# Decoder blocks on one core: attention stacks filled by copies inside SBUF, and Mamba's sum, decays and inputs later in the issue order

## What is computed

```python
# attention with 16 heads of 8 dims: L1x, L2x, L3x (keys and values of the context), L3a (rotated), softmax
scores = jnp.einsum('bhsd,bhtd->bhst', qh, kh) / scale
attn = jax.nn.softmax(scores, axis=-1)
out = jnp.einsum('bhst,bhtd->bhsd', attn, vh)
# L0a: causal linear attention, also with 16 heads of 8 dims (phi(x) = elu(x) + 1)
# L2a: Mamba, forward and backward in time, 256 channels, 16 states
def step(h, inp):
    d, b, c, ut = inp
    dA = jnp.exp(d[:, :, None] * A)
    h = dA * h + (d * ut)[:, :, None] * b[:, None, :]
    y = jnp.einsum('bdn,bn->bd', h, c)
    return (h, y)
```

## Time and profile before

| what | value |
|---|---|
| median of three runs | 4762.9 us (4759.52 to 4770.97) |
| the profiled execution, its own time | 4766.72 us |
| its span | 4764.2 us |
| PE busy | 3496.6 us (73%) |
| DVE busy | 2955.6 us (62%) |
| ACT busy | 1970.0 us (41%) |
| POOL busy | 1234.1 us (26%) |
| mean granted TensorE clock | 0.833 of full speed |
| moved by DMA | 328.00 MB, mean 69 GB/s |

### The profile page before, as it was taken

One profiled execution on the slowest core, in us unless ns is written; L12 is line 12 of the kernel. 1 busy time (PEld: TensorE's weight loads), 2 busy tenths in 40 slices (PEclk: granted clock), 3 DMA queues, 4 the chain that ended last, 5 costly groups with the idle time before them and its releaser, 6 DMA issues. The chain is left out here.

```text
span 4764.2 us, 69288 instructions
## 1 busy us (share of the span) xinstructions
PE 3496.6 (73%) x25546; PEld 2337.3 (49%) x25546; DVE 2955.6 (62%) x6919; ACT 1970.0 (41%) x3470; POOL 1234.1 (26%) x1568
## 2 busy tenths in 40 slices
PE   5868867666878878665886887856589698685674
PEld 3645635334665555433575654533357465352353
DVE  4436874884554785577545488477654548738646
ACT  2423545343343444543344355434235335443333
POOL 0001451550000243253000045145100005516410
PEclk7989978777988988777898998877789799786776
DMA  7110121313121021032122112122211200211321
GB/s 237 46 47 14 39 81 42 103 55 106 66 79 62 28 76 58 29 130 73 47 100 69 39 36 81 45 88 84 104 56 52 98 10 28 80 54 45 117 101 49
DMA packets 174905, 328.00 MB, mean 69 GB/s; under 512 B 13260, under 2 KB 114988, under 8 KB 173740
## 3 DMA queue, kind: packets, MB, share of 16 engines
q1 hardware_dynamic: 174572, 323.59, 20.1%
HBM read 231.87 MB, written 91.67 MB: 68 GB/s over the span
## 5 line engine op out<-in xcount | busy, mean ns | idle before, releaser
L1881 PE MATMUL bank<-sb_big,sb_weights_const 128*128 128x512 f32 x512 | 376.6, 826 | 333.9 <-DVE sb_big L2119 333.2
L1434 POOL TENSOR_TENSOR sb_rs<-sb_ve,sb_weights_const 128x4 f32<-128x4 f32 x112 | 113.4, 1012 | 1757.6 <-DVE sb_ve L1420 1757.3
L1997 POOL TENSOR_TENSOR sb_big<-sb_big 128x512 f32<-128x512 f32 x384 | 496.4, 1307 | 244.9 <-DVE sb_big L2097 244.3
L1958 ACT ACTIVATE bank<-sb_big,sb_Aneg 128x512 f32<-128x512 f32 x512 | 351.7, 689 | 497.4 <-DVE sb_big L2114 392.3
L1252 DVE TENSOR_REDUCE sb_small<-bank 128x4 f32<-128x308 f32 (+1 forms) x512 | 265.9, 523 | 344.5 <-PE bank L967 340.9
L2114 DVE TENSOR_TENSOR_SCAN sb_big<-bank,sb_big 128x512 f32<-128x512 f32 x384 | 464.6, 1210 | 6.6 <-ACT bank L1958 6.3
L988 PE MATMUL bank<-sb_big 128*77 128x128 bf16 (+1 forms) x2560 | 358.1, 234 | 83.7 <-DMA sb_big<-key_parts 30.3
L988 PEld LDWEIGHTS bank<-sb_big 128*77 128x77 bf16 (+1 forms) x2560 | 274.2, 117 | 140.2 <-issue 89.8
L967 PE MATMUL bank<-sb_big 128*128 128x77 bf16 (+1 forms) x2048 | 187.4, 227 | 179.5 <-DMA sb_big<-query_parts 114.2
L1677 PEld LDWEIGHTS bank<-sb_weights_L1f,sb_big 128*128 128x128 f32 x2048 | 257.3, 191 | 109.0 <-issue 104.9
L1137 ACT ACTIVATE sb_big<-bank 77x512 f32<-77x512 f32 (+1 forms) x352 | 207.9, 593 | 228.3 <-PE bank L1009 152.4
(11 more groups left out here) (344 smaller groups left out, 8111.7 us busy)
## 6 DMA issues: line engine op xcount, KB each, us to landing
sb_big<-query_parts SPq DMA_DIRECT2D x160, 512.0 KB, 6.5
sb_big<-state_rows SPq DMA_DIRECT2D x128, 512.0 KB, 3.8
query_parts<-sb_big SPq DMA_DIRECT2D x120, 384.0 KB, 3.3
sb_big<-key_parts SPq DMA_DIRECT2D x64, 512.0 KB, 8.9
sb_big<-context_key_parts SPq DMA_DIRECT2D x64, 308.0 KB, 3.6
key_parts<-sb_big SPq DMA_DIRECT2D x48, 384.0 KB, 4.1
context_key_parts<-sb_big SPq DMA_DIRECT2D x48, 231.0 KB, 4.1
sb_big<-masked_key_parts SPq DMA_DIRECT2D x32, 308.0 KB, 3.5
```

Source lines behind the costliest of these rows:

```text
L1881: pe.matmul(m.bank[s][2][:, :], m.const["ident"], M.h(s, 2 * (n % 2)), start=n == 0, stop=n == NS - 1)\
L1958: act.activation(M.dA(s, half), M.dl(s, half), ACT.Exp, scale=m.Aneg[:, NS * half + n:NS * half + n + 1])\
L1997: pool.tensor_tensor(M.h(s, 2 * (n % 2) + half), M.b_rows(s, n // 2)[:, n % 2, :], M.du(s, half), ALU.mult)\
```

## The change

Two things.

1. `heads_stack_sp` takes the place of `heads_write_sp` and `heads_read_sp`. When the parts are ready it copies them inside SBUF into the stack, nine DMAs of 8 destination partitions each, source 128 partitions of 1 KB (616 bytes for context keys), 128 KB each (77 KB); a tenth DMA reads the 56 rows below from DRAM (896 KB, 539 KB). Nothing is written to DRAM. PE waits once, before the first unit, for all ten of the queries and all ten of the keys.
2. In Mamba's timetable PE's sum goes from 0.6 to 0.9 of a state, ACT's decays of the next state from 0.4 and 0.9 to 0.6 and 1.1, POOL's inputs of the next state from 0.2 and 0.6 to 0.4 and 0.8.

```diff
@@ stacks(u), in heads_pe
-        if u % 4 == 0:
-            pe.wait_ge(*g.landed("rq%d" % (u // 4), A.key))
-            pe.wait_ge(*g.landed("rk%d" % (u // 4), A.key))
+        if u == 0:
+            pe.wait_ge(*g.landed("rq", (A.key, "below")))
+            pe.wait_ge(*g.landed("rk", (A.key, "below")))
@@
-def heads_write_sp(sp, g, m, A, name):
-
-    s = g.s
-    sp.wait_ge(*g.at("proj_d", (A.key, name, "low")))
-    dst = A.dram(s, name)[0:USED].rearrange("(i j d) h n -> (d h) i j n", i=3, j=3)
-    for copy in range(3):
-        sp.dma_start(dst[:, :, copy, :] if name == "q" else dst[:, copy, :, :], A.parts(s, name))\
-          .then_inc(*g.landing("w" + name, (A.key, copy)))
-
-
-def heads_read_sp(sp, g, m, A, name):
-
-    s = g.s
-    for each in name:
-        sp.wait_ge(*g.landed("w" + each, (A.key, 2)))
-    for group in range(4):
-        h = slice(4 * group, 4 * group + 4)
-        for each in name:
-            stack = A.q(s) if each == "q" else A.k(s)
-            sp.dma_start(stack[0:A.rows, h, :], A.dram(s, each)[0:A.rows, h, :])\
-              .then_inc(*g.landing(f"r{each}{group}", A.key))
+def heads_stack_sp(sp, g, m, A, name):
+
+    s = g.s
+    stack = A.q(s) if name == "q" else A.k(s)
+    sp.wait_ge(*g.at("proj_d", (A.key, name, "low")))
+    if name == "k" and A.masked:
+        sp.wait_ge(*g.landed("wm", A.key))
+    for i in range(3):
+        for j in range(3):
+            sp.dma_start(stack[8 * (3 * i + j):8 * (3 * i + j) + DH, :, :],
+                         A.parts(s, name)[:, i if name == "q" else j, :])\
+              .then_inc(*g.landing("r" + name, (A.key, i, j)))
+    sp.dma_start(stack[USED:A.rows, :, :], A.dram(s, name)[USED:A.rows, :, :])\
+      .then_inc(*g.landing("r" + name, (A.key, "below")))
@@ heads_sp
     for i, name in enumerate(names):
         yield A.time(A.split_at(i) + 1.1)
-        heads_write_sp(sp, g, m, A, name)
-    yield A.time(A.split_at(len(names) - 1) + 3.5)
-    heads_read_sp(sp, g, m, A, "".join(names))
+        heads_stack_sp(sp, g, m, A, name)
@@ mamba_pe
-            yield M.scan_at(way, n, 0.6)
+            yield M.scan_at(way, n, 0.9)
```

More of the change, by code:

```diff
@@ L227 @@
     rb1="an odd pair of rows of B is on all partitions",
[L228 to L232, removed]
+    wm="the masked keys' row is in DRAM",
+    rq="a copy of a query part is in its stack", rk="a copy of a key part is in its stack",
 )
@@ L1381, in heads_early_sp @@
         yield 0.01
[L1382 to L1386, removed]
+        heads_stack_sp(sp, g, m, A, "k")
 def heads_sp(sp, g, m, A):
@@ L1951, in mamba_act @@
             for half in range(2):
-                yield M.at(way, 0.13) if n == 0 else M.scan_at(way, n - 1, 0.4 + 0.5 * half)
+                yield M.at(way, 0.13) if n == 0 else M.scan_at(way, n - 1, 0.6 + 0.5 * half)
                 if n == 0:
@@ L1985, in mamba_pool @@
             for half in range(2):
-                yield M.at(way, 0.115) if n == 0 else M.scan_at(way, n - 1, 0.2 + 0.4 * half)
+                yield M.at(way, 0.115) if n == 0 else M.scan_at(way, n - 1, 0.4 + 0.4 * half)
                 if n == 0:
```

## The result

The changed kernel takes **5442.8 us** (median of 4 runs, 5431.6 to 5459.9) against 4761.2 us for the kernel before (4 runs, 4757.3 to 4771.0): 1.1435 times as long, 95% interval 1.1406 to 1.1463, or some 682 us more. The profiled execution took 5450.6 us, of which the span is 5448.8.

What follows compares the result with a forecast made beforehand. PE, busy 73%, is no bound by itself; late attention stacks stop both streams. 4766.7 + 391 (context layers) + 434 (both stacks) + 172 (clashes) - 45 (Mamba) = 5719 us profiled, forecast 5715 us, range 5000 to 6050.

Steps and rivals of the forecast that it cites:

- The forecast case: Whole kernel: copies at 54 GB/s delay the stacks; 5715 us, own range 5450 to 6050 us, chance 0.70.
- A microsecond of delay there is a microsecond of the span: First attention matmuls: engines run in order, so a late stack stops both streams and its delay counts in full.
- The rival in which half of the delay is covered: Stack waits: other work covers half the delay; 5070 us, sharing chance 0.06 with copies overlapping two by two.
- Two ways, 54 GB/s: Copies into 8 neighbouring partitions: two shared ways into SBUF at 27 GB/s each, 2.43 us per 131 KB copy.
- the first rival: Stack copies: writing into SBUF is not limited, stacks about 50 us faster together; 4670 us with Mamba, chance 0.13.
- The rival of copies that overlap two by two: Stack copies: engines running ahead use the next copy's ways too, 108 GB/s, 10.9 us a stack; 5070 us, chance 0.06.
- Half of the DMA engines: Stack copies: only 8 engines take part, 170 GB/s, 6.9 us a stack, +116 us; 4840 us, chance 0.07.
- the clash: Three places where both streams fill three stacks at once behind a context key stack: 85 us against 27.6, +172 us.
- The queue behind the context key stack: Context layers: queries' copies wait for the key stack ahead, 2.7 us on average; 8.7 us of it left in clashes.
- a third of PE's gain: Mamba: moving PE's sum removes up to 150 us of PE idle; -45 us taken, between -150 and +45.
- the late decay with VectorE's scan waiting: Mamba: 66 decays let one 0.69 us ACT step of the other stream pass while the scan waits, up to +45 us.
- Mamba's rows of B stand behind the copies ... so 0: DMA queue: rows of B wait up to 50 us, but their stream stands still then anyway, so nothing added.

Runs made afterwards that it cites:

- experiment 2: The changed kernel with Mamba's old timetable, so only the stacks are changed against the kernel before: 5499.0 us, ratio 1.1559.
- experiment 3: The changed kernel with each copy's eight destination rows 9 apart instead of neighbours: 4893.2 us, ratio 1.0301 to the kernel before.
- experiment 4: The changed kernel with eight copies going two by two into 16 neighbouring partitions, rows 2 apart, the ninth on eight neighbours: 5102.4 us, ratio 1.0729.
- experiment 10: The kernel before, old timetable, with each stack's three DRAM writes issued twice, first into spare memory nobody reads: 4929.7 us, ratio 1.0365.
- experiment 1: The kernel before, stacks still through DRAM, with only the three new numbers of Mamba's timetable: 4691.6 us, ratio 0.9866.

## Why the prediction was right, and where it was off

**The forecast case came.** 5715 us was forecast and 5443 measured, inside the range of 5000 to 6050 and 7 us below the forecast case's own 5450 to 6050. Slower is right, so is the mechanism; the stacks' part was some 240 us too large, all of its terms on the same side.

**"A microsecond of delay there is a microsecond of the span" held.** The read delays add to 759 us, the stacks alone cost 745 (experiment 2); in experiment 3 the same sum gives 21 x 4.6 + 12 x 8.8 + 3 x 3.9 = 214 us, less the timetable's 62 is 152, and 139 was measured; in experiment 4, 158 + 203 + 62 - 62 = 361 against 348. And it holds with the old stacks, 174 against 170 (experiment 10). The rival in which half of the delay is covered is excluded.

**"Two ways, 54 GB/s" was nearly right.** It was worked out from reading rates of 56 and 16 partitions and set to an unmeasured writing side. A stack's nine copies, with the rows below beside them, run at 57 GB/s (the mean 20.5 us) to 60, and copies alone at 60 to 75. So the price per stack was right to 6%, while the limit itself is not exactly 54: a way passes more than 27 GB/s, or neighbouring copies overlap a little, and nothing here tells which. The side is confirmed: the same bytes into other rows ran more than twice as fast (experiment 3), which no limit in the source, the engines or SP's issues explains, as these were the same. This also removes the first rival, in which the writing side is free. The rival of copies that overlap two by two, at 108 GB/s and 5070 us, falls with the 60 GB/s between the two stacks of a pair and with the windows of copies alone, none of which passes 75 GB/s. How many partitions share a way is not settled by this: the rows had said 5 to 7, and 16 neighbours being slower than rows 9 apart fits that as it fits 4.

In a sentence apart: the Trainium skill (SBUF — State Buffer, section "Door 1: The DMA port swizzle") puts four neighbouring partitions on a port and makes no difference between reading and writing; by an estimate from its 27.6 GB/s for one port, eight neighbours with two ports get 55 GB/s, 16 neighbours with four get 110, and rows 9 apart with eight get 221. The order of the three agrees with the runs; the 60 to 75 GB/s of copies alone lie above the first, the 108 to 121 agree with the second, and the 221 do not show, as the runs stop at 154 to 167.

**"Half of the DMA engines" was a wrong rival and a true mechanism.** It forecast 4840 us, as if nothing else limited. Where nothing else does, the share is 0.51 to 0.52 and the rate up to 167 GB/s against its 170 (experiment 3), at 4893 us with rows below last and 4845 us with them first. The Trainium skill (DMA: Bandwidth & Descriptors, section "Why a DMA increments its semaphore by 16 and not by 1") gives eight engines for sizes 128 and 8, and this trace agrees. With eight neighbours the share of copies alone is much the same, 0.56 to 0.60, at less than half of the rate: the share tells that DMA engines are occupied, not that they move data. The other engines were free for rows below.

**The terms that were too large.** The ready times forecast were 29.4, 51.5 and 85 us, and 24.7, 45.2 and 63.1 came. That is measured: 21 x 4.7 + 12 x 6.3 + 3 x 21.9 = 240 us too many, and the clash was off most for its size, 22 us of 85. How the excess divides among the prediction's steps is an estimate, for it needs a time for lead and landing, and no run shows the prediction's 1.9 us apart. With it, what came is 20.5 us for each stack and 2.3 us more outside clashes:

- Copies: 21.8 us a stack forecast, 20.5 came, over 21 + 24 + 9 = 54 stacks: 70 us too many.
- Rows below: 3 us for each stack, 162 us together; 2.3 us for each of 33 places, 76 us together, came. They run mostly beside the copies: 86 us too many.
- The queue behind the context key stack: 2.7 us in 21 layers and 8.7 in 3 clashes, 83 us together. Three stacks of 20.5 and the 1.9 make 63.4 us, and 63.1 was measured, which leaves nothing for it. Some of it exists: the three longest context layers, 26.4, 27.4 and 27.3 us, are ones whose key stack was issued only 9.3 to 9.4 us ahead, while with 14 us and more it is 24.1 to 25.8. The 2.7 us on the average was too much in any case.

**Mamba.** Forecast -45 us, measured -62.6 (experiment 1), inside -150 to +45. The step that was mis-sized is "a third of PE's gain": PE's idle time before the sum fell by 116 us and the span by 54% of it. The other half of the step, the late decay with VectorE's scan waiting, was no risk at all, since the scan waits for ACT 6 us in the whole kernel before; its row, shown at experiment 1, stands in the groups of before. The sign "more ACT idle before the decay" did come in the kernel after, 648.7 us against 497.4, but not from Mamba's timetable: the stacks alone raise it to 733.3 (experiment 2), and the timetable lowers it by 85 us, with the new stacks and with the old (497.4 to 412.3 in experiment 1).

**A term put at nothing.** "Mamba's rows of B stand behind the copies ... so 0": the wait came, 86.6 us of POOL and 29.4 of VectorE's scan behind it, and the 0 held, since the ready times alone account for the span.

**The account closes.** 4766.7 + 759 - 62.6 = 5463 us, and the profiled execution took 5450.6. The 13 us between are open, and sums of ready times come out 13 to 14 us above the measured cost in experiments 2, 3 and 4 as well; it may be cover at places that the means count as bare.

**The signs named beforehand.** PE idle about 20 us before the first use in a context layer (17.2 in the row above) and about 45 in the layers with both stacks (39.2), all engines silent, PE's share 64% against 61%: right. "GB/s near 54" in windows inside was a bad sign to name: most windows show 89 to 114, because the rows below run beside the copies, and those before the rows below start show 60 to 75.

**Slips in the working.** The first rival's own ready times make 21 x 1.3 + 12 x 1.5 + 3 x 7.6 = 68 us and not "about -50 us". The chances of the cases add up to 1.00, so the one-way rival "inside the tail" has none. Neither touches the forecast.

**What stays open.** Why eight neighbours run at 60 to 75 GB/s and not at 54, why a stack of copies into 16 neighbours adds 13.9 us where halving gives 11.4, and why SP needs 0.65 us to issue a copy, were not tried apart. A way to fill a stack from SBUF with copies that use all 16 DMA engines was not tried.

**The faster kernel.** Experiment 1, the timetable with the old stacks, is the fastest of all: 4691.6 us, 0.9866 of before. The change held a gain of 1.3% and a loss of 15.6%.

## What to carry to other kernels

Before replacing a round trip through DRAM by copies inside SBUF, ask how many ways into SBUF the destination partitions have and how many DMA engines the copy's sizes allow, and compare the whole chain from first issue to first use: here half of the memory traffic went away and the stacks came 2.3 to 3 times as late. Where eight partitions must be filled, spread them: rows 9 apart instead of neighbours was worth 550 us for one changed slice. In a timetable, move the step that the late engine waits for, and look in the groups which engine the others really wait for; moving ACT, which nobody waited for, changed nothing.

## What was not expected of the hardware

- Issuing one SBUF-to-SBUF copy of 131 KB takes SP 0.65 us (nine in 5.88), against 0.54 us for a write to DRAM of three times its bytes (three in 1.61). Nine issues alone are 5.9 us, two thirds of the whole old round trip. The prediction had assumed 0.4 to 0.5.
- SP is held back once a stack or more is queued: nine issues then take 17.8 to 19.7 us, about the copies' own time. Everything else that SP is to issue waits behind them.
- A copy with eight rows at the destination runs on eight of the 16 DMA engines, seen as a DMA share of 0.51 to 0.52 at 160 to 167 GB/s; where the read of the rows below is queued behind, the share rises to 0.66 to 0.93.
- With eight neighbouring rows the DMA engines are as busy (share 0.57) but move 60 to 75 GB/s: a busy share alone does not show a rate.
